# First expert block of a mixture-of-experts layer: its tokens found during the routing, its gather and products ahead of the slot list

## The reference

```python
flat = _layernorm(x)                                   # 1250 x 512
logits = flat @ router_w.T                             # 8 experts
topk_vals, topk_idx = jax.lax.top_k(logits, 2)
topk_w = jax.nn.softmax(topk_vals, axis=-1)
g = jnp.einsum('sd,edh->esh', flat, w_gate)            # 512 -> 1024
u = jnp.einsum('sd,edh->esh', flat, w_up)
y = jnp.einsum('esh,ehd->esd', jax.nn.silu(g) * u, w_down)
x = x + jnp.einsum('esd,se->sd', y, dense_w)           # two weights per node
```

## Time and profile before

| | |
|---|---|
| median of 3 runs | 1477.48 us (1475.59 to 1478.05) |
| profiled execution | 1477.98 us, its span 1476.1 us |
| mean granted TensorE clock | 0.958 of full speed |
| PE, DVE, POOL, ACT busy | 91%, 67%, 51%, 42% of the span |
| chain that ended last | PE 60%, POOL 21%, issue 8%, DMA 5%, DVE 4% |
| routing: choices found (L1701) | 1003.10 us |
| slots written (L1739) | 1010.10 us |
| first gather, first store of the list | 1014.97 and 1016.80 us |
| block 0, block 1, block 2 begin on PE | 1020.80, 1041.78, 1063.82 us |

### The profile page before, as it was taken

How to read it: one execution, slowest core, us unless ns; L and a number is a source line. 1 busy time by engine, 2 the same in 40 slices (tenths; PEclk the granted TensorE clock), 3 DMA queues, 4 the chain that set the end, 5 groups by cost and what they waited for, 6 DMA issues and landing times.

```text
span 1476.1 us, 29715 instructions
## 1 busy us (share of the span) xinstructions
PE 1341.4 (91%) x9251; PEld 652.1 (44%) x9252; DVE 988.3 (67%) x2487; ACT 624.1 (42%) x1097; POOL 751.9 (51%) x771
## 2 busy tenths in 40 slices
PE   6556999878889999999999999985999999999998
PEld 4233444435543333333333333474543454634445
DVE  7845766657847777777777777766565456556555
ACT  5445554655535666666666666571110111111010
POOL 4777777777767666666666666603511211221121
PEclk9777999988989999999999999997999999999999
DMA  5665333333239888888888888582351651524513
GB/s 200 229 213 167 117 115 110 117 118 111 100 105 317 259 257 255 257 257 256 257 255 259 256 257 256 159 338 71 78 192 29 199 185 29 199 80 136 197 29 96
DMA packets 125849, 262.62 MB, mean 178 GB/s; under 512 B 21041, under 2 KB 64776, under 8 KB 125115
## 3 DMA queue, kind: packets, MB, share of 16 engines
q0 software_dynamic: 48384, 141.37, 31.5%
q1 hardware_dynamic: 77410, 120.57, 24.5%
HBM read 204.35 MB, written 63.66 MB: 182 GB/s over the span
## 4 chain that ended last, share of the span: by engine, by line
PE 60%; POOL 21%; issue 8%; DMA 5%; DVE 4%; SPq 1%; ACT 1%; POOLq 0%; DVEq 0%; ACTq 0%
POOL edge_list L457 19%; PE psum L1380 19%; PE psum L1888 12%; PE psum L1908 8%; PE psum L1394 7%; PE psum L1389 5%; PE psum L1895 4%; DMA shared<-in_L_ffn_w_down 3%; PE psum L1373 3%; POOL slot_list L1806 1%; SPq L410 1%; DMA edge_list<-rec,place 1%; DMA slot_list<-pair,slots 1%; DMA node_table<-member 1%; DVE stats L1672 0%
## 5 line engine op out<-in xcount | busy, mean ns | idle before, releaser
L1265 POOL DMA_INDIRECT shared<-node_table,shared x328 | 310.4, 946 | 195.1 <-DVE msg L1346 103.5
L457 POOL DMA_INDIRECT edge_list<-rec,place x313 | 315.7, 1009 | 96.9 <-issue 95.1
L1348 DVE TENSOR_TENSOR msg<-shared,psum 128x768 f32<-128x768 f32 x328 | 310.1, 945 | 0.0
L1380 PE MATMUL psum<-wf,hT 128*32 128x512 f32 x2624 | 296.9, 592 | 0.8 <-ACT hT L1297 0.7
L1303 ACT COPY psum<-bias 128x512 f32<-128x512 f32 x328 | 193.3, 590 | 175.5 <-DVE msg L1348 154.2
L1346 DVE TENSOR_TENSOR msg<-shared,psum 128x256 f32<-128x256 f32 x328 | 135.8, 414 | 120.2 <-PE psum L1380 102.8
L1888 PE MATMUL psum<-shared,zT 128*64 128x512 f32 (+1 forms) x768 | 210.7, 594 | 3.9 <-DMA shared<-in_L_ffn_w_down 2.5
L1380 PEld LDWEIGHTS psum<-wf,hT 128*32 128x32 f32 x2624 | 84.7, 110 | 162.2 <-issue 134.9
L1840 POOL DMA_DIRECT2D ids<-slot_list x19 | 11.1, 584 | 279.0 <-DVE zN L1997 279.0
L472 PE MATMUL psum<-wf,fT 128*128 128x512 f32 (+1 forms) x158 | 95.9, 692 | 54.9 <-DVE rec L895 53.0
L1888 PEld LDWEIGHTS psum<-shared,zT 128*64 128x64 f32 (+1 forms) x768 | 77.0, 150 | 135.2 <-issue 128.7
(11 more groups left out here) (364 smaller groups left out, 1650.0 us busy)
## 6 DMA issues: line engine op xcount, KB each, us to landing
shared<-edge_list SPq DMA_DIRECT2D x332, 130.0 KB
shared<-in_L_ffn_w_gate SPq DMA_DIRECT2D x8, 2048.0 KB, 9.2
shared<-in_L_ffn_w_up SPq DMA_DIRECT2D x8, 2048.0 KB, 14.9
shared<-in_L_ffn_w_down SPq DMA_DIRECT2D x8, 2048.0 KB, 19.6
shared<-node_table,shared POOLq DMA_INDIRECT x328, 4.7
edge_list<-rec,place POOLq DMA_INDIRECT x313, 2.6
raw<-in_records SPq DMA_DIRECT2D x19, 256.0 KB, 3.8
xrow<-in_x SPq DMA_DIRECT2D x10, 250.0 KB
```

The costliest lines, as they stand in the source:

```text
L457: nc.gpsimd.indirect_dma_start(out=edge_list, out_offset=bass.IndirectOffsetOnAxis(ap=place[:n_, c:c + 1].bitcast(U32), axis=0), in_=rec[: ...
L1265: nc.gpsimd.indirect_dma_start(out=gat[:, k % G, :], out_offset=None, in_=table, in_offset=bass.IndirectOffsetOnAxis(ap=ix, axis=0)).then_ ...
L1348: nc.vector.tensor_tensor(m[:, 1:7, :].rearrange("p (a i) f -> p a i f", a=2), g[:, P:D].rearrange("p (i f) -> p i f", i=3).unsqueeze(1).t ...
L1380: ins = nc.tensor.matmul(WP[k % TS][q * W:(q + 1) * W, :], hT[:, (k // TS) % 2, at:at + W], wf2[:], start=False, stop=True, skip_group_che ...
```

## The change

The first block's tokens are found inside the routing. For expert 0 a rank needs no slots: it is the rank in the chunk plus the scanned count before the chunk. So right behind the scan DVE makes `rank0` (two operations) and the comparisons (`hits0`), PE multiplies (`find_tokens`, bank 5), and DVE reads the ids seven operations later. `zb` becomes another name for `bias`, which does not overlap the buffers of the routing; `first_ids` is allocated with the lasting buffers. The first expert gets at least two blocks of its own in `runs`, since PE's code for block 0 now stands ahead of the loop over the others. POOL gathers block 0 before it reads the number of blocks. DVE copies `zT` of block 0 first in the last stage and makes the pair weights and the other two comparisons behind it; PE does the two other searches inside block 0, behind GATE and behind UP, and DVE reads the third behind the first half's transposes.

```diff
+                def find_tokens(pe, n_, hits):
+                    for c in range(NC_):
+                        if c % (NC_ // 2) == 0:
+                            pe.wait_ge(picked_s, 2 * n_ + 1 + c // (NC_ // 2))
+                        for k in range(2):
+                            ins = nc.tensor.matmul(bank[5 + n_][:, 0:1], hits[:CR, c, :], tok_b[:CR, c, k:k + 1],
+                                                   start=(c == 0 and k == 0), stop=(c == NC_ - 1 and k == 1))
+                    ins.then_inc(ids_mm, 1)
+
+                def read_ids(dve, n_):
+                    dve.wait_ge(ids_mm, n_ + 1)
+                    nc.vector.tensor_copy(first_ids[:, n_:n_ + 1], bank[5 + n_][:, 0:1]).then_inc(ids_found, 1)
...
                         nc.tensor.matmul(bank[7][:CR, 0:NC_ * EX], const[:CR, C_TRI:C_TRI + CR], by_e, start=True, stop=True).then_inc(p_mm2, 1)
+                        find_tokens(pe, 0, hits0)
...
                         link(nc.vector.tensor_tensor_scan(before[:, 1:], bank[5][:, 0:NC_ * EX], zero80[:], 0.0, ALU.add, ALU.max))
+                        dve.wait_ge(p_mm2, 2)
+                        link(nc.vector.tensor_tensor(rank0[:CR, 0], bank[7][:CR, 0:NC_], before[:CR, 0:NC_], ALU.add))
+                        link(nc.vector.scalar_tensor_tensor(rank0[:CR, 1], rank0[:CR, 0], 1.0, mtot[:CR, :, 0], ALU.add, ALU.mult))
+                        for h_ in range(2):
...
+                            nc.vector.tensor_tensor(hits0[:CR, c0:c1, :], const[:CR, C_RANK:C_RANK + P].unsqueeze(1).to_broadcast(half_),
+                                                    rank0[:CR, 1, c0:c1].unsqueeze(2).to_broadcast(half_), ALU.is_equal).then_inc(picked_s, 1)
...
                         link(nc.vector.tensor_scalar(cnt_i[:], cnt_i[:], 1, None, ALU.bitwise_and))
+                        read_ids(dve, 0)
...
                         link(nc.vector.tensor_scalar(runs[:, :, 0], cnt_f[:], 0.5, 1.0, ALU.mult, ALU.max))
+                        link(nc.vector.tensor_scalar(runs[:, 0:1, 0], runs[:, 0:1, 0], 2.0, None, ALU.max))
...
-            zb = sbi("zb", [P, D])
+            zb = bias
...
                 def _(pool):
-                    nb = n_blocks(pool)
                     pool.sem_inc(turned, 1)
...
                     gather(first_ids[:, 0:1])
+                    nb = n_blocks(pool)
                     pool.wait_ge(routed, PAIRS)
...
+                    keep_busy(14)
                     pe.wait_ge(routed, STARTS)
                     first_run = read_row(pe, starts[0:1, 0:5], 0, NBLK)
-                    first_tokens(0)
-                    keep_busy(6)
-                    first_tokens(1)
-                    keep_busy(14)
+                    keep_busy(10)
...
                         hidden(GATE[0], wgate, 0)
+                        if search:
+                            find_tokens(pe, 1, pick[:, 0])
                         hidden(UP[0], wup, 0)
+                        if search:
+                            find_tokens(pe, 2, pick[:, 1])
...
                     ins.then_inc(turned, 1)
-                    first_tokens(2)
+                    keep_busy(6)
                     pe.wait_ge(w_in_s[0], 48)
+                    block_(0, alone(0), search=True)
                     for u in range(2):
-                        run_blocks(first_run[2 * u], first_run[2 * u + 1], alone(u))
+                        run_blocks(first_run[2 * u] if u else 1, first_run[2 * u + 1], alone(u))
...
                     link = dve_chain.on(dve)
-                    link(nc.vector.tensor_scalar(slot_f[:CR], slot_f[:CR], 1.0, None, ALU.add))
-                    in_block(0)
-                    picks(0)
+                    dve.wait_ge(turned, 2)
+                    nc.vector.tensor_copy(zT[:], Y[:].rearrange("p (j n) -> p j n", j=DJ)).then_inc(zt_done, 1)
                     dve.wait_ge(e_done, 1)
                     link(nc.vector.tensor_scalar(pair_sum[:CR], dd_keep[:CR], 1.0, None, ALU.add))
                     link(nc.vector.reciprocal(pair[:CR, 0, :, 1], pair_sum[:CR]))
                     nc.vector.tensor_tensor(pair[:CR, 1, :, 1], dd_keep[:CR], pair[:CR, 0, :, 1], ALU.mult).then_inc(routed, 1)
-                    next_block(1)
...
+                    link(nc.vector.tensor_scalar(slot_f[:CR], slot_f[:CR], 1.0, None, ALU.add))
+                    for n_ in range(1, 3):
+                        next_block(n_)
+                        picks(n_)
+                    read_ids(dve, 1)
```

More of the change, by code:

```diff
@@ L1858, in _ @@
                 def _(pe):
-                    def first_tokens(n_):
-                        for c in range(NC_):
-                            if c % (NC_ // 2) == 0:
-                                pe.wait_ge(picked_s, 2 * n_ + 1 + c // (NC_ // 2))
-                            for k in range(2):
-                                ins = nc.tensor.matmul(bank[5 + n_][:, 0:1], pick[:CR, n_ % 2, c, :], tok_b[:CR, c, k:k + 1],
-                                                       start=(c == 0 and k == 0), stop=(c == NC_ - 1 and k == 1))
-                        ins.then_inc(ids_mm, 1)
                     warm = const[:, C_ONE:C_ONE + P].bitcast(BF16)
@@ L1872, in keep_busy, with block_, hidden, hidden_turned @@
                             nc.tensor.matmul(bank[3][:, 0:2 * P], warm[:, 0:P], warm, start=True, stop=True)
+                    keep_busy(14)
                     pe.wait_ge(routed, STARTS)
                     first_run = read_row(pe, starts[0:1, 0:5], 0, NBLK)
[L1876 to L1879 removed]
+                    keep_busy(10)
+                    def block_(b, parts, search=False):
+                        whole = len(parts) == 1
+                        def hidden(dest, w, h_):
+                            for j in range(DJ):
+                                for lo, hi, u in parts:
+                                    ins = nc.tensor.matmul(dest[lo:hi, :], zT[:, j, lo:hi], w[u][:, j, h_ * D:(h_ + 1) * D],
+                                                           start=(j == 0), stop=(j == DJ - 1), skip_group_check=True)
+                            ins.then_inc(gu_mm, 1)
+                        def hidden_turned(dest, w):
+                            for q in range(DJ):
+                                for j in range(DJ):
+                                    ins = nc.tensor.matmul(dest[:, q * BLK:(q + 1) * BLK], w[parts[0][2]][:, j, D + q * P:D + (q + 1) * P], zT[:, j, :],
+                                                           start=(j == 0), stop=(j == DJ - 1), skip_group_check=True)
+                            ins.then_inc(gu_mm, 1)
+                        def turn_hidden(h_):
+                            pe.wait_ge(hid_done, b + 1)
+                            for q in range(DJ):
+                                ins = nc.tensor.transpose(TURNED[h_][:, q * BLK:(q + 1) * BLK], hid[:, h_, q * P:(q + 1) * P], ident)
+                            ins.then_inc(hid_turned, 1)
+                        def down(m):
+                            for lo, hi, u in parts:
+                                rows_ = hid[:, 1, (m - DJ) * BLK:(m - DJ + 1) * BLK] if whole and m >= DJ else hidT[:, m, lo:hi]
+                                ins = nc.tensor.matmul(Y[lo:hi, :], rows_, wdown[u][:, m, :],
+                                                       start=(m == 0), stop=(m == HM - 1), skip_group_check=True)
+                            if m == HM - 1:
+                                ins.then_inc(y_mm, 1)
+                        pe.wait_ge(zt_done, b + 1)
+                        hidden(GATE[0], wgate, 0)
+                        if search:
+                            find_tokens(pe, 1, pick[:, 0])
+                        hidden(UP[0], wup, 0)
+                        if search:
+                            find_tokens(pe, 2, pick[:, 1])
+                        if whole:
+                            hidden_turned(GATE[1], wgate)
+                            hidden_turned(UP[1], wup)
+                        else:
+                            hidden(GATE[1], wgate, 1)
+                            hidden(UP[1], wup, 1)
+                        pe.wait_ge(first_turned, b + 1)
+                        pe.wait_ge(y_bank, b + 1)
+                        for m in range(HM // 2 - 1):
+                            down(m)
+                        if whole:
+                            down(HM // 2 - 1)
+                            pe.wait_ge(hid_done, b + 1)
+                            pe.sem_inc(hid_turned, 1)
+                        else:
+                            turn_hidden(1)
+                            down(HM // 2 - 1)
+                            pe.wait_ge(hid_copied, b + 1)
+                        for m in range(HM // 2, HM):
+                            down(m)
@@ L1937, in alone @@
+                            block_(b, parts)
                     def alone(u):
@@ L2044, in gate, with block_ @@
```

(6 more changed lines are left out.)

70 lines of the change are left out of this document (7 added, 63 removed).

## The result

The changed kernel takes **1481.52 us** (median of 11 runs, 1478.72 to 1486.05), the kernel before 1478.05 (11 runs, 1475.59 to 1479.18): ratio **1.0026, interval 1.0016 to 1.0037**. It is slower by 3.5 us. The point lies inside the range of 1476.0 to 1481.8, but the forecast was no change, and this is one.

The account below looks back on a forecast made before the run. The slot list's stores on POOL, then the load of `to`, were taken to bound block 2's start, PE close behind. List 0.0 plus clock 1.6 on 1477.98 gave 1479.6, as a median 1479.1 us; range 1476.0 to 1481.8.

Parts of the forecast that it names:

- Gather, landing, copy: Start of block 0: gather at 1010.1, then landing, transposes and DVE's copy, so block 0 starts at 1015.4, 5.4 us earlier.
- The list's first store "where it was": POOL's first store of the slot list: now behind block 0's copy, yet still at 1016.8, as before.
- The bounds of −1.2 and +0.5: List's first store: −1.2 with the gather at 1008.85, +0.5 with block 0's transposes at the low clock.
- Its place is 1016.8 + 6.03 = 1022.8, so this costs nothing: POOL's second gather: the second search's ids let POOL go at 1021.4, before its place at 1022.8, so no delay.
- term list +0.0: The slot list's share of the sum: its end, and so block 2's start at 1063.8, does not move, 0.0 us.
- Rival 3: List's last entry lands sooner, being shared with SP's residual stores; block 2 starts 5.0 us earlier without gap: 1472.5, chance 0.08.
- The clock, +1.6: PE in block 2: after the longer gap the clock is halved for about 3 us, costing 1.6 (bounds 0 and 3.1).
- The gap, 5.0: PE ahead of block 2: block 1 ends at 1058.8, block 2 at 1063.8 waits for the list; 5.0 us idle, not 1.0.
- Rival 2: Low clock in block 0 makes the second search hold up the list: 1481.8; chance 0.2 together with slow clock recovery.
- its deciding point: GATE in block 0: the second search holds up the list when GATE lasts over about 5 us.
- by as much: Behind block 2 on PE: whatever moves block 2's start or rate moves the kernel's end by the same amount.
- rival 1: PE's clock holds at block 2, so the time is the list's alone: 1476.3 to 1478.0, at 1477.5; chance 0.2.

Follow-up runs that it names:

- e1: The changed kernel, unaltered, run again for a second profile: 1483.02 us, ratio 1.0032 to the kernel before.
- e3: The changed kernel with 14 warming matmuls on PE between block 1 and block 2: 1480.21 us, ratio 1.0011.
- e5: The changed kernel, with SP's ten stores of the residual waiting for the first gather instead of the second: 1476.13 us, ratio 0.9983.
- e7: The changed kernel, with DVE turning and copying block 2's rows before it waits for `to`: 1479.47 us, ratio 1.0015.
- e10: The changed kernel, with POOL's scattered sum of a block's rows put ahead of the gather for the next block: 1484.41 us, ratio 1.0045.
- e4: The changed kernel, with pair weights ahead of DVE's zT copy and the second gather behind eight list stores instead of four: 1480.23 us, ratio 1.0013.
- e2: The kernel before with one unused buffer of 12 bytes per partition where the change allocates `first_ids`: 1478.73 us, ratio 1.0003.
- e8: The kernel before, with DVE turning block 2's rows before it waits for `to`, and nothing of the change: 1478.30 us, ratio 1.0010.
- e9: e6 with 18 instead of 10 warming matmuls ahead of the first block's transposes: 1478.51 us, ratio 1.0001.
- e6: The changed kernel with the edits of e4 and e5 together: 1476.97 us, ratio 0.9992.
- e11: The kernel before, with SP's ten residual stores behind the first gather instead of the second, and nothing of the change: 1480.42 us, ratio 1.0009.
- e12: e9 with the second gather behind four of the list's stores instead of eight: 1474.80 us, ratio 0.9976.

## Why the prediction was wrong, step by step

- **Gather, landing, copy.** Put at 7.0 us after the product (1010.1 − 1003.1); measured +7.80 and, in e1, +7.26. The landing, 3.97, took 4.56 and 3.48. The transposes, taken at the full rate, ran at the low clock in both profiles (1.12 and 1.04). Each step held to within a microsecond, but block 0 began at +14.55 and, in e1, at +12.65, where the sum put it at +12.3 (1015.4 − 1003.1).
- **The list's first store "where it was".** +15.05 in the profile of the result, +13.35 in e1, against +13.70. The bounds of −1.2 and +0.5 hold the second; the first lies 0.85 beyond, by the gather's start and landing.
- **The failed step: "Its place is 1016.8 + 6.03 = 1022.8, so this costs nothing", and with it the term list +0.0.** The second gather came at +21.99, and in e1 at +20.29, where it was at +19.73; block 2 began 0.84 and 1.66 later. Two things were missed.

  First, the comparisons for the second and third search now run on DVE beside POOL's second and third store, and those stores take 1.55 and 1.78 us: the second gather moves 0.91 in every profile of the unaltered order (after, e1, e3, e5, e7, e10). The Trainium skill has this in "SBUF — State Buffer", section on who interferes with whom: a DVE instruction with two SBUF inputs contends with a GpSimd instruction that reads SBUF. The rows agree in part: the kernel before has it too, at its first gather (1.53 against 0.98), which begins while DVE compares, but its next two stores, 1.22 and 1.23 long, pass beside another comparison unstretched. The first of these stores was under way before that comparison began (1016.80), and the second began in its last 0.2 us (1018.32); both stores that were stretched in the changed kernel began with 0.5 to 0.7 us of a comparison left. That the comparisons cause the stretch is read from these overlaps; no run moved them alone.

  Second, the first store was taken for what sets the list's end. It isn't: e4 moved that store 2.8 us ahead of its old place and DVE's scaling came at +55.0, where it was at +54.8. The end hangs on SP's residual stores, which start with the second gather, and e5 shows it by moving those alone. With the list in the changed order (after, e1, e3, e7, e10) `to` is issued at +52.3 to +53.4, with it in the old one (before, e2, e8) at +49.8 to +51.7. How much of that is the stretch and how much the later first store is not separated: it doesn't grow in step with the second gather's delay (2.26 in the profile of the result, 0.56 in e1), and the scatter seen in e2 is as large.

  DVE's comparisons of the kernel before, at its first gather and at its first two stores:

```profile
1014.10 1.55 DVE L2006 TENSOR_TENSOR pick<-const,rank_in 125x640 bf16<-125x640 f32 x2
...
1016.93 1.56 DVE L2006 TENSOR_TENSOR pick<-const,rank_in 125x640 bf16<-125x640 f32 x2
```

- **Rival 3** had that mechanism ("shared with SP's ten stores of the residual") and was dismissed by "SP's stores still start with the second gather's landing, which stays where it was". It didn't stay; and the sharing was priced as a possible gain only, never as a loss.
- **The clock, +1.6.** Right: 1.70, in e1 1.90, in e3 1.70. It fell after gaps of 2.01, 3.31, 5.44 and 6.55 us ahead of block 2 (after, e3, e10, e1) and of 4.28 ahead of block 1 (e9), but not in e4 after 3.79, so the length of the gap alone doesn't tell.
- **The gap, 5.0.** 6.55 in e1, where block 1 ends at +55.8, as forecast (1058.8 − 1003.1 = 55.7), and block 2 is late. 2.01 in the profile of the result: there block 0 began 1.9 later than in e1 and ran GATE, its first half, at the low clock (5.50 for x8, 3.67 in e1), so block 1 ended 3.7 later, and block 2 began 0.8 earlier.
- **Rival 2** named 1481.8 and missed the way there: the x8 row lasted 5.50, past its deciding point, yet the fourth store ended at 1028.70 and the gather followed 0.30 later, so POOL did not wait for the second search.
- **Not in the sum:** 0.94 ahead of block 4. The prediction let block 2 move the end "by as much"; it moved by 1.3 more, this wait and 0.4 in later ones. In the kernel before, e2 and e8 the wait is absent; after, e1, e4, e5, e6, e7 and e10 have 0.8 to 1.0; e3, e9, e11 and e12 have 0.15 to 0.26. POOL's next gather goes with it: it follows the first of the three weight loads by 1.1 to 1.4 us in the six of the first group that keep POOL's order, by 2.0 to 2.5 in the seven others. But e10 put that gather 4.5 behind and kept the wait, so this is a sign, not a shown cause; the cause stays open.

With the terms as measured, 0.84 + 1.70 + 0.94 + 0.4 = 3.9 us, the two profiled executions are accounted for. The forecast had 0.0 + 1.6 of it: the clock came as it said, the list and the weights did not. The cause of the clock's part and of the wait ahead of block 2 is shown by e5, which removes both; that of the rest isn't.

The range's low end, too, has a slip: the earliest list with the clock held is 1476.3 by rival 1's own figure, and the range begins at 1476.0.

## What to carry to other kernels

When a step is moved to an earlier place, follow also the transfers that are released by it on queues that the change doesn't touch: here ten stores on SP, put behind a gather, decided whether a small load on POOL came in time. The same short load took 2.0 us in the median and 5.86 beside a stream here, so price a short transfer at the end of a chain by what else is in flight when it is issued. And where work is interleaved by hand over three queues, an order that removes one wait can bring up the next: of the variants timed here, only the one that joins three edits (those of e4, e5 and e9, with the gather in its old place) was clearly faster than the kernel before. Which of the three it could do without was not tried.

## What the runs showed of the hardware that I had not expected

- A 1 KB load took 5.86 us until its reader moved (e4) beside another queue's stores at 119 to 127 GB/s, at a third of the DMA engines' share; the median of all twenty such loads in the profile of the changed kernel is 2.0 us from issue to landing.
- POOL's indirect stores stretch from 1.2 to 1.55 and 1.78 us where they begin while DVE compares (after). One in e12 did not, though it began at 1017.59, in the middle of two comparisons that ran from 1016.87 to 1018.44: it took 1.18, and DVE's next small operation 0.38 instead of 0.17.
- The first indirect gather of 256 KB took from 3.37 (e6) to 4.58 us (e5) from issue to the transposes that waited for it, and the second one 9.46 in e9 among the residual's stores (issued 1024.58, turned from 1034.04).
